# Writing out the experts' loops of the last three batches and interleaving the whole program anew on four engines

## The reference

```python
qkv = x @ w_qkv.T                      # split in heads, tokens put in snake order
scores = einsum('bhsqd,bhskd->bhsqk', qh * scale, kd)   # 4 segments of 128 queries, 64 keys each
attn = softmax(scores); o = einsum('bhsqk,bhskd->bhsqd', attn, vd); out = o @ w_out.T
x = x + layernorm(attention(layernorm(x)))

probs = softmax(xf @ router_w); topw, topi = top_k(probs, 2)
h = silu(einsum('nd,edf->nef', xf, w1)); ye = einsum('nef,efd->ned', h, w2)
routed = einsum('ne,ned->nd', combine, ye)              # combine holds the two weights
shared = sigmoid(xf @ shared_gate_w) * (silu(gate) * up @ shared_down)
x = x + layernorm(routed + shared)
```

## Time and profile before

| | us |
|---|---|
| median of 3 runs (lowest, highest) | 154.2 (154.0, 155.8) |
| the profiled execution's own time | 153.29 |
| its span, first to last instruction | 151.5 |
| PE busy (share of the span) | 136.9 (90%) |
| DVE busy | 124.0 (82%) |
| ACT busy | 106.9 (71%) |
| POOL busy | 56.9 (38%) |

### The profile page before, as it was taken

How to read it: one execution, slowest core, us unless ns; L and a number is a source line. 1 busy time by engine, 2 the same in 40 slices (tenths; PEclk the granted TensorE clock), 3 DMA queues, 4 the chain that set the end, 5 groups by cost and what they waited for, 6 DMA issues and landing times.

```text
span 151.5 us, 3493 instructions
## 1 busy us (share of the span) xinstructions
PE 136.9 (90%) x1120; PEld 117.2 (77%) x1120; DVE 124.0 (82%) x481; ACT 106.9 (71%) x254; POOL 56.9 (38%) x55
## 2 busy tenths in 40 slices
PE   6989979998999999999999999999899999699800
PEld 4678766786977889778798999999789997699600
DVE  6969998698999899988967628899999269957693
ACT  3888788867968685878799857668847676468600
POOL 6453030000093109802720299296304973023011
PEclk9999999999999999999999999999999999999985
DMA  4850199969992930000000000000020002000202
GB/s 145 242 139 2 48 165 130 261 128 154 218 277 88 165 42 4 2 4 0 2 0 4 0 0 4 0 2 0 2 74 2 0 0 75 1 0 0 69 0 69
DMA packets 13217, 9.54 MB, mean 63 GB/s; under 512 B 1040, under 2 KB 12048, under 8 KB 13200
## 3 DMA queue, kind: packets, MB, share of 16 engines
q1 hardware_dynamic: 12784, 9.12, 28.5%
q10 hardware_dynamic: 416, 0.21, 0.5%
HBM read 3.69 MB, written 1.05 MB: 31 GB/s over the span
## 4 chain that ended last, share of the span: by engine, by line
PE 64%; DVE 18%; ACT 6%; DMA 5%; issue 3%; SPq 2%; POOL 1%; DVEq 0%; ACTq 0%
PE bank L646 13%; PE bank L523 9%; PE bank L540 6%; DMA Qs<-qcl 5%; PE bank L500 5%; PE bank L408 4%; PE bank L411 4%; DVE X L1448 4%; PE bank L413 3%; PE bank L412 3%; PE bank L573 3%; PE bank L553 2%; DVE ST L1224 2%; PE bank L483 1%; PE bank L559 1%
## 5 line engine op out<-in xcount | busy, mean ns | idle before, releaser
L340 POOL TENSOR_TENSOR RS<-VE,nhalf 128x4 f32<-128x4 f32 x14 | 15.4, 1100 | 55.0 <-DVE VE L1232 54.8
L1448 DVE SCALAR_TENSOR_TENSOR X<-bank,CW,X 128x128 f32<-128x128 f32 x80 | 22.5, 342 | 10.9 <-PE bank L646 10.8
L646 PEld LDWEIGHTS bank<-w2n,Pr 128*128 128x128 f32 x192 | 24.9, 191 | 3.0 <-ACT Pr L1037 1.1
L646 PE MATMUL bank<-w2n,Pr 128*128 128x128 f32 x192 | 25.2, 275 | 0.6 <-ACT Pr L1037 0.6
L1328 DVE TENSOR_REDUCE negm<-bank 128x8 f32<-128x512 f32 x32 | 21.1, 685 | 2.9 <-PE bank L500 2.3
L1037 ACT ACTIVATE Pr<-bank 128x512 f32<-128x512 f32 x27 | 16.2, 604 | 7.9 <-PE bank L413 7.8
L972 ACT ACTIVATE Pr<-bank 128x512 f32<-128x512 f32 x32 | 18.7, 598 | 3.9 <-PE bank L523 3.6
L523 PE MATMUL bank<-Qs,Kb 128*128 128x128 f32 x128 | 19.5, 280 | 0.6 <-ACT Pr L972 0.3
L523 PEld LDWEIGHTS bank<-Qs,Kb 128*128 128x128 f32 x128 | 16.5, 191 | 3.2 <-issue 1.6
L315 POOL TENSOR_TENSOR EX<-base,DL 128x36 f32<-128x36 f32 x2 | 12.2, 6125 | 8.8 <-DVE DL L1381 8.8
L411 PE MATMUL bank<-XH,w1h 128*128 128x512 f32 x32 | 15.2, 474 | 0.0
(11 more groups left out here) (150 smaller groups left out, 308.5 us busy)
## 6 DMA issues: line engine op xcount, KB each, us to landing
Qs<-qch SPq DMA_DIRECT2D x6, 256.0 KB, 5.6
Kb<-kone SPq DMA_DIRECT2D x8, 128.0 KB, 5.2
X<-in_L_attn_x SPq DMA_DIRECT2D x4, 256.0 KB, 6.6
XP<-in_x_snake SPq DMA_DIRECT2D x3, 256.0 KB, 4.1
Ks<-kch SPq DMA_DIRECT2D x6, 128.0 KB, 3.4
Qs<-qcl SPq DMA_DIRECT2D x3, 256.0 KB, 7.2
out<-XN SPq DMA_DIRECT2D x3, 256.0 KB, 2.2
w1n<-in_L_ffn_w SPq DMA_DIRECT2D x1, 512.0 KB, 9.2
```

Of the source, the lines that this page charges most:

```text
L340: nc.gpsimd.tensor_tensor(RS[:, k, b], VE[:, k, b], nhalf[:], ALU.pow).then_inc(pw[k], 1)
L646: i = mm(ps[output_bank(n, s)][:, s * P:(s + 1) * P], lhs[:, s * P:(s + 1) * P], w, start=True, stop=True)
L1448: V.scalar_tensor_tensor(out=acc[:, b, t], in0=ps[output_bank(n)][:, t * P:(t + 1) * P], scalar=CW[:, b, t, k:k + 1], in1=acc[:, b, t], op ...
```

## The change

No step is added or removed: the functions are the same, except that POOL's last two powers get a function of their own. All four blocks call them in a new order, in the attention too, and the loops over batches 1 to 3 are written out, so that each step stands where it is put and not where the loop puts it for all batches. The numbers of steps of each kind are as before. SP's order isn't changed.

```diff
@@ POOL
-            key_columns(0)
             powers(0, 3)
+            key_columns(0)
...
             powers(1, 0)
+            add_rows(0)
+            experts_low()
+            shared_low()
             key_columns(3)
...
@@ PE, start
             warm_up(6, TH)
+            x_T_0(0)
             warm_up(1, TH)
-            x_T_0(0)
             qkv_0(0)
@@ PE, end of the attention of batch 0
             attend(0, 3)
-            values(2)
             attend_T(0, 2)
             attend_T(0, 3)
+            values(2)
+            output_T(0)
             max_T(1)
-            output_T(0)
-            scores_k(1, 0, (0,))
             project(0)
-            scores_k(1, 0, (1,))
...
+            scores_k(1, 0)
@@ PE, experts
-            for b in range(1, B):
-                if b == 1:
-                    project(B - 1)
-                expert_h(b, 0)
-                shared_o(b)
-                for e in range(E):
-                    if e + 1 < E:
-                        expert_h(b, e + 1)
-                    elif b + 1 < B:
-                        gate(b + 1)
-                        up(b + 1)
-                    expert_o(b, e)
-                    if b == 1 and e == 6:
-                        moe_in(B - 1)
-                    if b == 1 and e == 7:
-                        router(B - 1)
...
+            expert_h(2, 0)
+            expert_h(2, 1)
+            expert_o(1, 7)
+            expert_h(2, 2)
+            moe_in(3)
+            shared_o(2)
+            expert_o(2, 0)
+            expert_h(2, 3)
+            router(3)
...
+            expert_o(2, 6)
+            gate(3)
+            up(3)
+            expert_o(2, 7)
+            expert_h(3, 0)
+            expert_h(3, 1)
+            expert_h(3, 2)
+            shared_o(3)
+            expert_h(3, 3)
+            expert_o(3, 0)
+            expert_h(3, 4)
+            expert_o(3, 1)
+            expert_o(3, 2)
+            expert_o(3, 3)
...
@@ ACT, start
-            key_ones()
             normalise_x_0(0)
...
             q_rows_0(0, 1)
-            normalise_x(1, (3,))
+            key_ones()
             k_rows_0(1)
@@ DVE, experts of batches 1 and 2
+            accumulate(0, 7)
+            router_sums(2)
             spread_y(3)
             gather(1, 3)
...
+            accumulate(2, 4)
+            finish(1)
+            accumulate(2, 6)
+            router_sums(3)
+            gated(3)
+            router_inverse(3)
+            accumulate(2, 7)
+            probabilities(3)
...
```

More of the change, by code:

```diff
@@ new lines, in _ @@
+            shared_o(1)
+            expert_h(1, 1)
+            expert_h(1, 2)
+            expert_o(1, 0)
+            expert_h(1, 3)
+            expert_o(1, 1)
+            expert_h(1, 4)
+            expert_o(1, 2)
+            expert_h(1, 5)
+            expert_o(1, 3)
+            expert_o(1, 4)
+            expert_h(1, 6)
+            expert_h(1, 7)
+            gate(2)
+            expert_o(1, 5)
+            expert_o(1, 6)
+            up(2)
+            expert_h(2, 0)
+            expert_h(2, 1)
@@ L1193, in _ @@
             silu(0, 7)
+            silu(1, -1)
             o_copy(3)
[L1196 to L1214 removed]
+            silu(1, 0)
@@ L1217, in _ @@
+            silu(3, 6)
+            finish_out(2)
+            silu(3, 7)
+            last_shift()
         @block.vector
@@ new lines, in _ @@
+            spread_r(3)
+            accumulate(1, 2)
+            gather(2, 3)
+            accumulate(1, 4)
+            neg_mean(2, 3)
+            accumulate(1, 6)
+            chosen(2)
+            gated(2)
+            neg_mean(1, 2)
+            combine(2)
+            accumulate(1, 7)
+            add_other(1)
+            x3_low(3)
+            finish(0)
+            norm_out(1)
+            logits(3)
+            expert_weights(2)
+            largest_logit(3)
+            below_largest(3)
@@ L1711, in _ @@
+            finish(2)
+            accumulate(3, 2)
+            accumulate(3, 4)
+            add_other(3)
+            accumulate(3, 5)
+            accumulate(3, 6)
+            last_expert()
             last_out(0)
```

480 lines of the change are left out of this document (240 added, 240 removed).

## The result

| | before | after |
|---|---|---|
| median of the runs beside each other (lowest, highest), us | 154.2 (154.0, 155.8) | 148.5 (148.4, 148.8) |
| ratio, 95% interval | | 0.961 [0.955, 0.968] |
| a second series, median, us | 153.5 | 149.0 |
| ratio there | | 0.970 [0.968, 0.973] |
| the profiled execution's own time, us | 153.29 | 148.80 |

The forecast was 150.3, 3.9 us less than before. The first series has 5.7 less, the second and the two profiled executions 4.5. In the first series the kernel before was slower than in any other (its medians in the later ones: 153.5 to 153.8), so 4.5 to 5 is the better figure. Runs in which TensorE's clock fell for long are left out of all comparisons of times.

The account below looks back on a forecast made before the run. PE was taken to bound the kernel, so only its waits, start and tail could be won: -0.4 - 0.8 - 2.7 = -3.9 makes 153.29 into 149.4, plus 0.9 to the median gives 150.3 us (own range 148.4 to 151.6).

Parts of the forecast that it names:

- The start, -0.4: Up to batch 1's scores: kone leaves its place ahead of the first tiles, scores start at 27.4, not 27.82.
- The bound of +1.0 for kone's four DMAs: Worst case at the start: kone's four DMAs drain behind one another and push the queries' DMA, 1.0 us lost.
- The middle, -0.8: From 27.8 to 94.5, attention with batch 0's experts: PE's waits, including 0.5 on divide, shrink by 0.8 us.
- The last stage, -2.7: From 94.5 to the end, experts of batches 1 to 3: removed PE waits win about 2.7 us.
- (a): End of batch 2: gated(3) no longer waits behind batch 3's whole router on DVE; PE's 1.46 us wait goes.
- (c): End of the experts: both last silus go ahead of last_shift on ACT; PE's 0.65 us wait goes.
- (d): Around 105 to 115: spread waits for batch 3's norm and copies shrink as moe_in(3) comes later, 0.8 us won.
- (b): POOL's power for batch 3's router starts later, at 118 to 119.5; cost 0 to 1.5 us, taken as 0.2.
- The tail, 0: Behind 143.2: 8.3 us of DVE, POOL and the last DMA keep the same instructions, no change.
- First, exchanged waits: PE's waits in attention and experts are merely exchanged for others, no change of note: 152.3 us, chance 0.16.
- Second, the long power holds DVE: POOL's 6.12 us power blocks DVE's products of two SBUF tiles, up to 5.3 us lost: 155.6, chance 0.06.
- Third, the clock: Start: warm-ups end too early to raise PE's clock, work up to about 12 doubles, 4.5 us: 154.8, chance 0.04.

Follow-up runs that it names:

- kone_first: Changed kernel with ScalarE's key_ones back ahead of the first normalised tiles: 149.6 us, ratio 0.969 to the kernel before.
- two_waits_only: Kernel before with two moves: most of batch 3's router behind gated(3), and last_shift at ACT's end with finish_out(2) ahead of the last silu: 151.0 us, ratio 0.984.
- new_attn_old_experts: New order up to project(3), the old expert loops of the kernel before behind it: 153.3 us, ratio 0.997; 153.6 in a repeat.
- after_router_back: Changed kernel with batch 3's router on VectorE again in one piece ahead of accumulate(2, 6) and gated(3): 151.0 us, one run.
- after_again: The changed kernel once more, unchanged, for another profile: span 147.4 us, against 147.0 in its first profile.
- router3_only: Kernel before with only batch 3's router moved on VectorE, behind accumulate(2, 6) and gated(3): 152.1 us, ratio 0.987.
- shift_only: Kernel before with only ScalarE's order changed, finish_out(2) ahead of batch 3's last silu and last_shift behind the silus: 152.9 us, ratio 0.993.
- warm_more: Changed kernel with four more warm-up matmuls ahead of the first transposes: 148.4 to 149.7 us in three runs, ratio 0.972.

## Why the prediction was right or wrong

**The bound and the direction.** Right. PE bounds, its work is the same, and in the last stage, where most of the gain lies, the gain is what PE waited for.

**The start, -0.4.** The keys' DMA came at 16.88, not 16.4, and batch 1's scores at 27.86, not 27.4. Counted from the constants it is -0.73, at the good end of the bounds. The place of kone moves the first transposes by 1.21 (2.95 against 1.74), and the times of kone_first fit that this is the gain; the keys' DMA itself isn't seen there without the clock's fall. The bound of +1.0 for kone's four DMAs didn't come: they end at 16.76, just ahead of the keys', and cost some 0.15. But the 0.76 by which the constants were used later took it back in the profile. The prediction took 4.35 for a constant of the kernel; it differs between executions of one kernel by up to 0.5, and, on average, between the two programs. Nothing in the one trace could show that.

**The middle, -0.8.** -0.95. The wait on `divide` went. The wait that was feared at `attend_T` of batch 0 (some 0.3) is 0.14, at 34.91; the 0.50 on `AVs` in batch 1 was not foreseen. Between batch 1's scores and `project(3)` the idle time that the profile shows fell only from 1.18 to 1.06. The other 0.8 lies in time that counts as busy, and no run splits it up: the size came out right, its parts beyond `divide` stay open. `project(3)` was to start at 93.3 and started at 94.37: 0.76 of that for the constants, 0.79 for the hidden step that now stands ahead of it and that the text had forgotten, less 0.48 of gain over the forecast.

**The last stage, -2.7.** This is the step that failed by its size, with the right mechanism: -3.48 measured (-3.60 with the old attention). It counted 3.5 us that aren't work, and that count was right; the split of it wasn't. (a) and (c) were priced by the lengths in brackets, 2.11, and two_waits_only has 2.45 for them. Each wait costs its bracket and 0.17 us, as the busy time ahead of it holds the last matmul to its modelled end; the four waits of the stage (1.46, 0.65, 0.4, 0.2) hold 0.68 of hidden time beside their 2.68 of visible time. (d), taken as 0.8 of a rest of 1.2 (by its own numbers 3.5 - 2.11 = 1.4), is 3.60 - 2.45 = 1.15; 0.9 of that are the two small waits with their 0.17, the rest has no row. (b), taken as 0.2 lost, lost nothing: the power began at 117.22, ahead of the 118 that was its earliest, and ran to 123.34; DVE asked at 124.81. (a) had two slips that cost nothing. `expert_h(3, 2)` isn't cover for `gated(3)`, as it waits for it; `gated(3)` ended at 125.86, 1.35 us ahead of it. And the slack ahead of `expert_o(3, 3)`, said to be 0.2 to 0.3, is 0.95 (`accumulate(3, 0)` ended at 131.90, the outputs began at 132.85). The last outputs start at 137.61 against 142.01, and DVE takes the last accumulates from 138.70, where 139.3 was forecast. The safe reading of "3.5 aren't work" would have been: an order that leaves no bracket gives all 3.5.

**The tail, 0.** -0.11.

**The sum.** -0.4 - 0.8 - 2.7 = -3.9 stands against -0.73 - 0.95 - 3.48 - 0.11 + 0.76 = -4.5. For the profiled execution 149.4 was forecast and 148.80 came. The 0.9 that was added to reach the median of 154.2 was the second step that failed, and the larger one: that series was high for the kernel before and not for the changed one, whose median of 148.54 lies 0.26 below its profiled execution. Of the 1.8 us between 150.3 and 148.5 it makes 1.2, the stages 0.6.

**The rivals.** First, exchanged waits: fell, the last stage is idle for 0.00. But new_attn_old_experts is much like this rival: of an early gain of 1.4 its last stage gives 1.17 back. Second, the long power holds DVE: fell. `finish(1)`'s X rows, two inputs in SBUF, lie inside POOL's power of 117.22 and take what they always take, while the product CW beside POOL's multiplication of 99.09 took 1.02 in place of 0.19; rows of the changed kernel's DVE and POOL:

```profile
99.16 1.02 DVE L1501 SCALAR_TENSOR_TENSOR CW<-EQ,PB 128x32 f32<-128x32 f32 x1
...
122.40 0.35 DVE L1567 SCALAR_TENSOR_TENSOR X<-X,RS,TR 128x128 f32<-128x128 f32 x1
```

```profile
99.09 1.04 POOL L321 TENSOR_TENSOR TR<-Y,RS 128x512 f32<-128x512 f32 x1
```

The price of this blocking is real, though, for additions and multiplications: it made the router of after_router_back 2.0 us longer. Third, the clock: in the changed kernel's two profiles it rose at 6.6 and 5.4 and stayed up. Two profiles of its variants show a fall all the same, from the other side than feared: not warm-ups too short to raise the clock, but a clock raised early, warm-ups used up, a wait of 2.2 to 2.3 us, and a fall. (Behind waits of 1.0, 1.5 and 1.6 us at this place, in after_again, router3_only and shift_only, there was none there.) That the wait is the cause is argued from these rows; warm_more, built to test it, didn't decide. It costs 1.7 to 2.1 us, not 4.5, and the kernel before has executions at a like mean clock (155.2 to 156.0 at 0.973 to 0.978), of which no profile was kept.

## What to carry to other kernels

When counted work and measured time of a stage differ, price an order that removes the waits at the whole difference, not at the waits' listed lengths: each hides the end of the last matmul ahead of it, here 0.17 us. Cut two profiles at the row where the first DMA is used before comparing absolute times, and compare the kernel before over several series: here these two were worth 0.8 us and up to 0.7 us, as much as most terms of the sum. And move a whole in-order queue with the engine it feeds: of 1.4 us gained early on TensorE 0.2 to 0.5 were left where ScalarE's and VectorE's steps of batch 3 stood at their old places.
